# Low-rank transposes spread over later tiles, block numbers loaded by ScalarE, and another parity of the output rows' two buffers

## The chip, the core and the metric

The kernel runs on one core of one Trainium2 chip. The metric is the time of one execution on the device in microseconds (us). TensorE (PE) multiplies; its weight loads are recorded apart (PEld). VectorE (DVE), ScalarE (ACT) and GpSimd (POOL) do the elementwise work. SyncE (SP) computes nothing and issues most of the DMAs; ScalarE issues some.

## What is computed

Four residual layers over x of shape (32, 32, 512), 1024 rows of 512 in all:

```python
def reference(x, ...):
    x = x + _L0_cond_ref(x, itok_B_0_15, L0_cond_weights)      # per block of 32 rows: einsum('bct,bcd->bdt', x, weights[condition])
    x = x + _L1_cond_ref(x, itok_B_0_2, W, lora_A, lora_B_w)   # x @ W.T + 0.5 * (x @ lora_A[label]) @ lora_B_w.T
    x = x + _L2_cond_ref(x, L2_cond_weight, itok_B_3_7)        # x @ weight[adapter].T
    x = x + _L3_cond_ref(x, ...)                               # attention: q, k, v, norm, rope, 512 cached keys, 32 heads, Wo
    return x
```

In L0, L1 and L2 each of the 32 blocks picks its weights by a number that is given with the input. L3 is an attention with 32 query heads and 8 key heads over pages of a cache, and an output projection by Wo of 512 x 4096.

## The kernel before

The 1024 rows are eight tiles (TT) of 128 rows, four blocks (BT) of 32 to a tile; a row of 512 is four chunks (KC) of 128. Each engine has its own program, written out by hand, and engines wait for each other on semaphores. Products that need full precision are split into a high and a low part and done in three passes (`three_pass`, lines 107 to 111).

`stage_layers` does L0, L1, L2 and the tables of sines and cosines for L3. The list `uses` (lines 202 to 211) sets the order in which TensorE fills its eight PSUM banks, one bank to an entry, in turn; entry n waits until entry n-8 has been drained. TensorE, ScalarE and VectorE all walk through this list, so it sets the order of all three. Its entries are, for tile t: L0 (the product of L0), x1T (x turned), low (x times lora_A, line 372 on), lowT (the low-rank rows turned, line 382), L1 (the product of L1 with a last product of lowT with bw_t, line 392), x2T, L2 (line 402) and x3T.

On VectorE, `low` is two steps (lines 601 and 604), `lowT` a copy into low_t (line 608), and L0, L1, L2 an add to x (line 579). At the entry L1(0), ahead of its add, VectorE computes the angles (lines 507 to 518) and their reduction (lines 523 to 529), then reads block numbers and copies the first adapter weights (line 537). ScalarE at the same entry takes the sines (line 461) and copies its share of weights (line 434). GpSimd makes eight tables from the sines (line 341), after clearing and scaling bw_t (lines 330 and 333). These steps live in w1n, the room into which SP later fetches adapter weights: `fetch(0)` (line 291) waits for all eight tables, `fetch(1)` and `fetch(2)` for the last L1 product. L2(0) waits for the first fetch, L2(1) for the second.

At the start, SP issues the two rows of block numbers (lines 275 and 276), then x in four parts (line 280) and the weights of the later steps. ScalarE issues the table of L0's weights w0_all (line 418). VectorE and ScalarE wait for both rows of numbers and the table, then copy the blocks of L0's weights into place (lines 549 and 424), 16 copies each, four to a tile.

`stage_project_attend_output` projects, attends and multiplies by Wo. Between the attention and the end there are 32 units of output, four to a tile. For each unit SP loads the attention's rows and their scales (`load_o`, line 1021; `load_inv`, line 1027) into one of two buffers in room_a (`o_slot`), GpSimd multiplies them (line 1176), ScalarE takes the high part (line 1728), VectorE the low part (line 1537), and TensorE does 24 products (lines 109 to 111). The load of unit u+2 waits until the low part of unit u is done (o_lo_done). Unit 2 alone has a third buffer; unit 3 follows unit 1 in buffer 1. In the first units the high and low parts of Wo are made too (lines 1717 and 1521), from loads at line 653.

## Time and profile before

| | us |
|---|---|
| median of 3 runs | 1190.09 |
| lowest and highest | 1187.87, 1191.71 |
| the profiled execution | 1188.03 |
| its span | 1186.2 |
| TensorE busy | 1166.4 (98%) |
| VectorE busy | 851.5 (72%) |
| ScalarE busy | 687.1 (58%) |
| GpSimd busy | 727.6 (61%) |
| DMA, mean over the span | 239 GB/s |

The profile is of one execution. Its page gives the busy time of each engine; the timeline gives instructions in order of time, with the idle time ahead of an instruction and what released it in brackets. TensorE's granted clock is full throughout. A TensorE product is recorded with its whole length through the array, so consecutive ones overlap.

### The profile page before, as it was taken

The page shows a single profiled execution, that of the slowest core. Times are in us where ns is not written, and L with a number is a line of the kernel's source. Part 1 is how long each engine was busy: PE and PEld are TensorE (multiplying, and loading weights), DVE is VectorE, ACT ScalarE, POOL GpSimd, SP SyncE. Part 2 cuts the span into 40 slices and gives each one's busy share as a digit, 9 for nine tenths or more (in the row PEclk, how much of TensorE's full clock was granted, in tenths as well). Part 3 has the DMA queues.
Part 4 walks back from the last instruction along what each step waited for, and adds up shares of the span by engine and source line. Part 5 has one row for each costly group of instructions (what it writes and reads, how often), then busy time and mean ns, then how long its engine had stood idle before and what let it go on. Part 6 is the DMA issues. An engine that isn't in the chain of part 4 may idle for free.

```text
span 1186.2 us, 27883 instructions
## 1 busy us (share of the span) xinstructions
PE 1166.4 (98%) x8138; PEld 1030.1 (87%) x8138; DVE 851.5 (72%) x1746; ACT 687.1 (58%) x1647; POOL 727.6 (61%) x566
## 2 busy tenths in 40 slices
PE   7999999999999899999999999999999999999998
PEld 5746888888888799999999999999999998787877
DVE  7878687777866977877878778887788878722222
ACT  4175444344444577777777777777777778412111
POOL 1403999999999765555555555555555556344442
PEclk9999999999999999999999999999999999999999
...
GB/s 340 137 279 196 147 134 134 143 82 133 133 125 190 169 256 304 293 298 302 297 301 298 292 304 295 302 296 294 304 295 301 291 334 323 267 218 208 223 212 115
DMA packets 254401, 283.67 MB, mean 239 GB/s; under 512 B 56053, under 2 KB 208629, under 8 KB 254358
## 3 DMA queue, kind: packets, MB, share of 16 engines
...
HBM read 236.78 MB, written 46.27 MB: 239 GB/s over the span
## 4 chain that ended last, share of the span: by engine, by line
PE 52%; POOL 21%; issue 7%; DMA 5%; DVE 3%; ACT 2%; SPq 0%; ACTq 0%; POOLq 0%; DVEq 0%
PE early_pair L1237 19%; PE early_pair L1212 10%; PE early_pair L109 7%; PE early_pair L110 6%; PE early_pair L111 6%; POOL prj_rstd L1146 6%; POOL prj_qn L1148 5%; POOL prj_ta L1136 5%; DMA all_room_a<-inv_scratch 5%; PE early_pair L1244 3%; POOL prj_rs L1140 3%; POOL all_room_a L1176 2%; DVE out_o_lo L1537 2%; ACT out_o_hi L1728 1%; DVE out_wo_lo L1521 1%
## 5 line engine op out<-in xcount | busy, mean ns | idle before, releaser
L1604 ACT ACTIVATE att_prob<-att_neg,att_nmax 128x544 f32<-128x544 f32 x256 | 192.1, 750 | 115.9 <-DVE att_nmax L1369 91.0
L1369 DVE CUSTOM_DVE_ANT_1 att_neg<-att_mask,early_pair 128x576 f32<-128x576 f32 x256 | 192.1, 751 | 83.3 <-PE early_pair L111 67.5
L1156 POOL TENSOR_TENSOR att_k_lo<-all_room_a,att_k_hi 128x544 fp32r<-128x544 f32 x123 | 165.8, 1349 | 135.4 <-ACT att_k_hi L1630 135.4
L1156 POOL TENSOR_TENSOR att_k_lo<-att_kT,att_k_hi 128x544 fp32r<-128x544 f32 x128 | 173.9, 1359 | 105.5 <-ACT att_k_hi L1630 105.5
L1421 DVE COPY att_pT<-early_pair 128x512 f32<-128x512 f32 x256 | 175.8, 687 | 28.3 <-PE early_pair L1212 28.3
L109 PE MATMUL early_pair<-att_k_hi,att_q_lo 128*128 128x288 f32 (+1 forms) x512 | 168.8, 330 | 1.5 <-DVE att_nmax L1369 1.5
L1212 PE MATMUL early_pair<-all_ident,att_prob 128*128 128x128 f32 x1024 | 157.0, 276 | 0.0
L110 PE MATMUL early_pair<-att_k_lo,att_q_hi 128*128 128x288 f32 (+1 forms) x512 | 147.4, 288 | 0.0
L111 PE MATMUL early_pair<-att_k_hi,att_q_hi 128*128 128x288 f32 (+1 forms) x512 | 147.2, 288 | 0.0
L1176 POOL TENSOR_TENSOR all_room_a<-all_room_a 128x1024 f32<-128x1024 f32 x31 | 78.9, 2545 | 98.7 <-DMA all_room_a<-inv_scratch 98.7
L1237 PE MATMUL early_pair<-att_pT,att_vc 128*128 128x128 f32 x1024 | 135.4, 275 | 0.6 <-ACT att_ost L1761 0.6
L1237 PE MATMUL early_pair<-att_pT,all_room_b 128*128 128x128 f32 x1024 | 135.3, 275 | 0.0
L1212 PEld LDWEIGHTS early_pair<-all_ident,att_prob 128*128 128x128 f32 x1024 | 116.3, 140 | 20.9 <-issue 13.6
L1641 ACT ACTIVATE prj_sq<-early_pair 128x512 f32<-128x512 f32 x64 | 38.3, 599 | 165.5 <-PE early_pair L111 161.4
L1237 PEld LDWEIGHTS early_pair<-att_pT,att_vc 128*128 128x128 f32 x1024 | 124.5, 192 | 0.9 <-ACT att_ost L1761 0.8
L1237 PEld LDWEIGHTS early_pair<-att_pT,all_room_b 128*128 128x128 f32 x1024 | 124.5, 192 | 0.0
L1537 DVE TENSOR_TENSOR out_o_lo<-all_room_a,out_o_hi 128x1024 fp32r<-128x1024 f32 x31 | 41.1, 1325 | 107.7 <-ACT out_o_hi L1728 107.7
L1136 POOL TENSOR_TENSOR prj_ta<-prj_ta,prj_tb 128x640 f32<-128x640 f32 x64 | 101.1, 1579 | 9.1 <-DVE prj_tb L1471 9.0
L109 PE MATMUL early_pair<-out_wo_hi,out_o_lo 128*128 128x512 f32 x256 | 101.1, 395 | 2.5 <-DVE out_o_lo L1537 2.4
L1728 ACT ACTIVATE out_o_hi<-all_room_a 128x1024 fp32r<-128x1024 f32 x31 | 32.8, 1060 | 120.9 <-POOL all_room_a L1176 120.9
L111 PE MATMUL early_pair<-out_wo_hi,out_o_hi 128*128 128x512 f32 x256 | 99.8, 390 | 0.0
L110 PE MATMUL early_pair<-out_wo_lo,out_o_hi 128*128 128x512 f32 x256 | 99.8, 390 | 0.0
(164 smaller groups left out, 2928.7 us busy)
## 6 DMA issues: line engine op xcount, KB each, us to landing
all_room_a<-in_k_cache_t SPq DMA_DIRECT2D x256, 128.0 KB, 5.9
att_kT<-in_k_cache_t SPq DMA_DIRECT2D x256, 128.0 KB, 6.8
...
q_scratch<-prj_qst SPq DMA_DIRECT2D x64, 256.0 KB
att_vc<-in_L_cond_v_cache SPq DMA_DIRECT2D x128, 128.0 KB, 4.0
att_vc<-in_L_cond_v_cache ACTq DMA_DIRECT2D x128, 128.0 KB, 5.1
all_room_a<-o_scratch SPq DMA_DIRECT2D x31, 512.0 KB, 3.8
all_room_a<-inv_scratch SPq DMA_DIRECT2D x31, 512.0 KB, 5.5
```

The source lines that it names most:

```text
L109: pe.matmul(out, w_lo, x_hi, start=first, stop=False)
L110: pe.matmul(out, w_hi, x_lo, start=False, stop=False)
L111: return pe.matmul(out, w_hi, x_hi, start=False, stop=last)
L1136: g.tensor_tensor(ta[s][:], ta[s][:], tb[s][:], ALU.add).then_inc(pool_step, 1)
L1146: g.tensor_tensor(rstd[s][:], rs[s][:], power[:], ALU.pow).then_inc(pool_step, 1)
L1156: g.tensor_tensor(k_lo[j % SPLITS][:], kT[j // HK % 2][:, :, j % HK, :], f32(k_hi[j % SPLITS][:]), ALU.subtract).then_inc(k_split, 1)
L1176: g.tensor_tensor(o_n[s], o_n[s], inv_rows[s], ALU.mult).then_inc(o_scaled, 1)
L1212: t = pe.transpose(bank[:, c * P:(c + 1) * P], p[:, c * P:(c + 1) * P], ident[:])
L1237: pe.matmul(o, vc[s][:, c, cols], pT[j % 2][:, c, :], start=(c == 0 and j % PAIR == 0), stop=False)
L1369: v.tensor_tensor_reduce(halves[0], halves[1], scores_of(j, n)[:, :, 0:KA], 1.0, 3.0e38, ALU.add, ALU.min, nmax[j % 2][:]).then_inc(maxed, 1)
L1421: v.tensor_copy(pT[j % 2][:], pt[bank_of(j)][:].rearrange("p (c q) -> p c q", c=NCH)).then_inc(kept, 1)
L1604: act.activation(prob[j // GROUP % 2][:, j % GROUP, :], neg[j % 2][:, 0:KEYS], ACT.Exp, bias=nmax[j % 2][:, 0:1], scale=-1.0, accum_out=to ...
```

## The change

Four edits. First, the order of `uses`: lowT(t-3) follows low(t) from t = 3 on, and the last three follow L1(0). Since all three engines walk the list, VectorE's copies move with them, and the angles (and on ScalarE the sines) are now attached to L1(1). In L1 the waits for lowT and bw_t stand ahead of the last product only. Second, low_t no longer lies in the room that a_n, a_hi and a_lo had, which are still read by the later low products; it lies in a part of w2a. Third, ScalarE issues the two rows of block numbers, one ahead of w0_all and one behind it. Fourth, output unit 3 goes to buffer 0, unit 4 to buffer 1 and so on; its load waits for o_lo_done 1 instead of 2.

```diff
-        low_t = after_a.sb("low_t", [P, TT, P])
+        FETCHED = BT - 1
+        low_t = [w2a[:, i // KC, FETCHED, i % KC * P:(i % KC + 1) * P] for i in range(TT)]
@@ uses
-        uses += [("low", t) for t in range(TT)]
-        uses += [("lowT", t) for t in range(TT)]
-        uses += [("L1", t) for t in range(TT)] + [("x2T", 0)]
+        for t in range(TT):
+            uses += [("low", t)] + ([("lowT", t - 3)] if t >= 3 else [])
+        uses += [("L1", 0)] + [("lowT", t) for t in range(TT - 3, TT)]
+        uses += [("L1", t) for t in range(1, TT)] + [("x2T", 0)]
@@ SP
-                sp.dma_start(idx[:, 0, :], inp["itok_B_0_15"].rearrange("(a b) -> a b", a=1)).then_inc(idx_in, 16)
-                sp.dma_start(idx[:, 1, :], inp["itok_B_3_7"].rearrange("(a b) -> a b", a=1)).then_inc(idx_in, 16)
@@ TensorE, L1
-                        pe.wait_ge(lowt_ready, i + 1)
-                        pe.wait_ge(bw_ready, 1)
                         tok = slice(i * P, (i + 1) * P)
...
-                        end(u, pe.matmul(bank[:], low_t[:, i, :], bw_t[:], start=False, stop=True))
+                        pe.wait_ge(lowt_ready, i + 1)
+                        pe.wait_ge(bw_ready, 1)
+                        end(u, pe.matmul(bank[:], low_t[i], bw_t[:], start=False, stop=True))
@@ ScalarE
+                act.dma_start(idx[:, 0, :], inp["itok_B_0_15"].rearrange("(a b) -> a b", a=1)).then_inc(idx_in, 16)
                 act.dma_start(w0_all, inp["w0_t"]).then_inc(w0_all_in, 16)
+                act.dma_start(idx[:, 1, :], inp["itok_B_3_7"].rearrange("(a b) -> a b", a=1)).then_inc(idx_in, 16)
...
-                    elif kind == "L1" and j == 0:
+                    elif kind == "L1" and j == 1:
                         act.wait_ge(reduced, 2)
@@ VectorE
-                    if u == ("L1", 0):
+                    if u == ("L1", 1):
                         angles()
@@ output
         def o_slot(it, i):
-            return 2 if at_first(it) and i == 2 else i % 2
+            return i if at_first(it) and i <= 2 else (i + 1) % 2
+
+        def o_count(it, i):
+
+            return 1 if at_first(it) and i <= 2 else it * (O_UNROLL // 2) + (i + 1) // 2
@@ SP
                 sp.wait_ge(o_lo_done, 1)
-                sp.sem_inc(o_in[0], 16)
-                sp.sem_inc(inv_in[0], 16)
-                sp.wait_ge(o_lo_done, 2)
                 load_o(0, 3)
                 load_inv(0, 3)
+                sp.wait_ge(o_lo_done, 2)
                 load_o(0, 4)
                 load_inv(0, 4)
@@ GpSimd
-                    if s == 2:
-                        pool.wait_ge(o_in2, 16)
-                        pool.wait_ge(inv_in2, 16)
-                    else:
-                        pool.wait_ge(o_in[s], (it * (O_UNROLL // 2) + i // 2 + 1) * 16)
-                        pool.wait_ge(inv_in[s], (it * (O_UNROLL // 2) + i // 2 + 1) * 16)
+                    pool.wait_ge(o_in2 if s == 2 else o_in[s], o_count(it, i) * 16)
+                    pool.wait_ge(inv_in2 if s == 2 else inv_in[s], o_count(it, i) * 16)
```

VectorE's order at the end of the low-rank stage, before (lay_low_own and lay_low are the two steps of `low`, lay_low_t the copies of `lowT`, lay_row_i the first step of the angles):

```order
L601 SCALAR_TENSOR_TENSOR lay_low_own<-lay_lab_of,lay_lab,early_pair 128x160
L604 TENSOR_REDUCE lay_low<-lay_low_own 128x32
L608 COPY lay_low_t<-early_pair 128x128 x8
L507 TENSOR_SCALAR lay_row_i<-lay_pos_i 128x1
L508 CAST lay_base<-lay_row_i 128x1
L512 CAST lay_pos<-all_len_i 32x8 x4
```

The same place on VectorE after (all_room_a is x, so line 580 is the add of L1(0)):

```order
L602 SCALAR_TENSOR_TENSOR lay_low_own<-lay_lab_of,lay_lab,early_pair 128x160
L605 TENSOR_REDUCE lay_low<-lay_low_own 128x32
L609 COPY lay_w2a<-early_pair 128x128
L580 TENSOR_TENSOR all_room_a<-all_room_a,early_pair 128x512
L609 COPY lay_w2a<-early_pair 128x128 x3
L508 TENSOR_SCALAR lay_row_i<-lay_pos_i 128x1
L509 CAST lay_base<-lay_row_i 128x1
L513 CAST lay_pos<-all_len_i 32x8 x4
```

The add of L1(0) and three of the eight copies now stand between the last `low` and the angles; the other copies stand in the low-rank stage.

ScalarE's order at the start, after (before, lay_w2a, the table w0_all, stood alone ahead of the reading of the numbers from lay_idx):

```order
L417 DMA lay_idx<-in_itok_B_15 1x32
L418 DMA lay_w2a<-in_w_t 128x512
L419 DMA lay_idx<-in_itok_B_7 1x32
L262 TENSOR_LOAD lay_idx
L425 ISA
```

SP's queue at the start of the output stage, before (L653 loads Wo, L1021 rows, L1027 scales; units 3 and 4 stand behind one wait):

```order
L653 DMA out_wo5_2526<-in_wo_t 128x4x512 [waits pa_scored]
L1021 DMA all_room_a<-o_scratch 128x4x256 [waits pa_o_lo_done]
L1027 DMA all_room_a<-inv_scratch 128x4x256
L1021 DMA all_room_a<-o_scratch 128x4x256
L1027 DMA all_room_a<-inv_scratch 128x4x256
L653 DMA out_wo6_2527<-in_wo_t 128x4x512 [waits pa_exped]
```

The same place after (L654, L1026 and L1032 are the same loads):

```order
L654 DMA out_wo5_2526<-in_wo_t 128x4x512 [waits pa_scored]
L1026 DMA all_room_a<-o_scratch 128x4x256 [waits pa_o_lo_done]
L1032 DMA all_room_a<-inv_scratch 128x4x256
L1026 DMA all_room_a<-o_scratch 128x4x256 [waits pa_o_lo_done]
L1032 DMA all_room_a<-inv_scratch 128x4x256
L654 DMA out_wo6_2526<-in_wo_t 128x4x512 [waits pa_exped]
```

Each of the two units now has a wait of its own, unit 3 for o_lo_done 1 and unit 4 for o_lo_done 2.

## Rows read from the trace of the kernel before

**Rows 1.** Page, busy us (share of the span) and instructions of each engine.
```profile
PE 1166.4 (98%) x8138; PEld 1030.1 (87%) x8138; DVE 851.5 (72%) x1746; ACT 687.1 (58%) x1647; POOL 727.6 (61%) x566
```
**Rows 2.** Timeline, first 10 us: start, length, engine, line, operation [idle before, releaser].
```profile
0.72 0.35 SPq L275 DMA_DIRECT2D lay_idx<-in_itok_B  x1
1.43 1.95 SPq L280 DMA_DIRECT2D all_room_a<-in_x  x4
...
0.72 0.39 ACTq L418 DMA_DIRECT2D lay_w2a<-in_w_t  x1
...
4.99 3.01 DVE L549 COPY early_tabs<-lay_w2a 32x32 f32 x16 [4.99 <-issue]
...
6.27 3.75 PE L365 MATMUL early_pair<-all_room_a,early_tabs 128*128 128x512 f32 x4 [6.27 <-DMA all_room_a<-in_x]
```
**Rows 3.** DMA view, 0 to 8 us in 40 slices; issues, KB, us to landing.
```profile
GB/s 0 0 0 0 0 0 0 0 62 154 51 164 399 379 288 215 348 307 338 287 307 215 123 246 328 184 307 246 297 317 389 328 358 287 389 358 389 348 358 389
...
lay_w2a<-in_w_t ACTq DMA_DIRECT2D x1, 256.0 KB, 2.7
...
all_room_a<-in_x SPq DMA_DIRECT2D x1, 512.0 KB, 4.7
```
**Rows 4.** Timeline of TensorE, from the low-rank transposes to the end of L1(0).
```profile
30.62 0.94 PE L382 MATMUL early_pair<-all_ident,lay_low 128*128 128x128 f32 x7
...
33.19 0.47 PE L109 MATMUL early_pair<-lay_w,early_xT_lo 128*128 128x512 f32 x1 [1.08 <-DVE lay_low_t L608]
...
36.02 1.02 PE L392 MATMUL early_pair<-lay_bw_t,lay_low_t 128*128 128x512 f32 x2
```
**Rows 5.** Timeline of the other engines, from the copies to the first fetch.
```profile
31.58 1.66 DVE L608 COPY lay_low_t<-early_pair 128x128 f32<-128x128 f32 x8
...
34.44 0.75 DVE L512 CAST lay_pos<-all_len_i 32x8 f32<-32x8 int32 x4 [0.95 <-DMA lay_w1n<-in_L_cond_k_norm_w]
...
44.93 1.15 ACT L461 ACTIVATE lay_w1n<-lay_w1n 128x512 f32<-128x512 f32 x2 [15.51 <-DVE lay_w1n L529]
...
46.16 10.94 POOL L341 TENSOR_TENSOR early_tabs<-lay_w1n 128x512 f32<-128x512 f32 x8 [13.12 <-ACT lay_w1n L461]
...
57.28 0.40 SPq L291 DMA_DIRECT2D lay_w1n<-in_w_t  x1
```
**Rows 6.** DMA view: the first fetch, and the second and third.
```profile
lay_w1n<-in_w_t SPq DMA_DIRECT2D x1, 1024.0 KB, 5.5
...
lay_fetched<-in_w_t SPq DMA_DIRECT2D x2, 1024.0 KB, 6.7
```
**Rows 7.** Timeline: the last add of L1, and the first weight load of L2.
```profile
62.46 0.69 DVE L579 TENSOR_TENSOR all_room_a<-all_room_a,early_pair 128x512 f32<-128x512 f32 x1 [2.94 <-PE early_pair L392]
...
63.56 0.15 PEld L402 LDWEIGHTS early_pair<-lay_w2a,lay_low 128*32 128x32 f32 x4 [0.51 <-DVE all_room_a L579]
```
**Rows 8.** SP's queue ahead of output unit 3, and the landing of wo's fourth load.
```profile
995.94 0.75 SPq L653 DMA_DIRECT2D out_wo<-in_wo_t  x1
...
1004.78 0.37 SPq L1021 DMA_DIRECT2D all_room_a<-o_scratch  x1
...
out_wo<-in_wo_t SPq DMA_DIRECT2D x1, 1024.0 KB, 13.2
```
**Rows 9.** Timeline of GpSimd and VectorE around output unit 3.
```profile
1012.20 2.71 POOL L1176 TENSOR_TENSOR all_room_a<-all_room_a 128x1024 f32<-128x1024 f32 x1 [10.50 <-DMA all_room_a<-inv_scratch]
1016.38 3.00 POOL L1176 TENSOR_TENSOR all_room_a<-all_room_a 128x1024 f32<-128x1024 f32 x1 [1.47 <-DMA all_room_a<-inv_scratch]
...
1012.57 4.56 DVE L1521 TENSOR_TENSOR out_wo_lo<-out_wo,out_wo_hi 128x1024 fp32r<-128x1024 f32 x2
1017.05 3.41 DVE L1537 TENSOR_TENSOR out_o_lo<-all_room_a,out_o_hi 128x1024 fp32r<-128x1024 f32 x1
```
**Rows 10.** Timeline of TensorE: the starts of output units 3 and 5.
```profile
1020.52 0.50 PE L109 MATMUL early_pair<-out_wo_hi,out_o_lo 128*128 128x512 f32 x1 [0.82 <-DVE out_o_lo L1537]
...
1033.03 0.50 PE L109 MATMUL early_pair<-out_wo_hi,out_o_lo 128*128 128x512 f32 x1 [1.07 <-DVE out_o_lo L1537]
```

3 lines of the change are left out of this document (1 added, 2 removed).

## The prediction

> **What bounds the kernel now.** I read the page first: TensorE is busy for 98% of the span [rows 1], so only what moves TensorE's idle time or its start and end can show. The change adds and removes no work of weight (the eight transposes, copies and loads are the same), so the sum is about waits. I then read the order of the changed kernel, and went to the three places where it differs: the first 10 us (timeline and DMA view), 30 to 64 us (timeline by engine), and 1000 to 1035 us, where the output stage starts. What lies between (projection and attention, some 900 us) is untouched, and everything there waits for its predecessor and for nothing at a fixed time, so a shift at its front is carried to the end.
>
> In the front stage TensorE waits three times for something that the change touches. It starts at 6.27, released by the landing of x [rows 2]. It pauses between the transposes of the low-rank rows, which start at 30.62, and the first L1 product at 33.19 [rows 4]. And the first L2 product loads its weights at 63.56 [rows 7]. In the output stage it waits 0.82 us before unit 3 and 1.07 us before unit 5 [rows 10].
>
> **The change, part by part.**
>
> (1) The block numbers. Before, SP issues both index loads from 0.72 on and x from 1.43; ScalarE issues the table of weights w0_all at 0.72 [rows 2]. After, x is issued at 0.72, so 0.71 earlier; w0_all follows one index load (0.35 us of issue), and the second index load follows w0_all. VectorE's placing of the blocks waits for all three. w0_all landed 2.7 us after its issue, that is at 3.4, while x had the engines only for the last part of this, and the traffic from 2 us on is some 300 GB/s [rows 3]. Now 256 KB of w0_all and the first 512 KB of x are in flight together from about 1.7 on: 768 KB at 300 GB/s end at 4.3, and the index load ends behind the w0_all part of them. The table and both numbers are there somewhere between 0.4 us later than before (the issue alone) and 1.5 us later (all of x's first part ahead of them). I take 1.0. So VectorE's copies start at 6.0 instead of 4.99; four of the 16 (3.01 us [rows 2]) make a tile, so TensorE's first product starts at 6.8, not 6.27: **+0.55 us**, called d below, from -0.15 to +1.05. That x lands at 5.4 instead of 6.1 (4.7 us after issue [rows 3]) is of no use, since it is no longer what comes last. A pure gain of 0.7 is a rival below. The tile loop behind it runs on VectorE's adds and splits, one after another, so d goes through.
>
> The Trainium skill, DMA: Bandwidth & Descriptors, section on queues, rings and completion order, says that each ring's descriptors are taken in order and that an engine drains a packet of one queue row before it turns to another; it speaks against this part: the index load would stand behind w0_all in ScalarE's ring and both behind x's share. By it d would be at its upper end, 1.05, and the sum 0.5 us more; the rows show only that the two queues share one rate.
>
> (2) The transposes. Before, eight in one run from 30.62 and eight VectorE copies from 31.58, 1.66 us in all, then L1(0) at 33.19 [rows 4, 5]. After, five stand in the low-rank stage or right behind it, 0.12 us each (0.94 for seven), so L1(0) starts at 30.62 + 0.6 = 31.2: 2.0 earlier. Its last product starts 2.83 later [rows 4], at 34.0. bw_ready, which GpSimd makes behind the last low product, is asked for only there, 2.8 us into L1(0), and I take it as hidden. Three transposes follow L1(0), 0.35 us. L1's eight tiles then end 2.0 - 0.35 = 1.65 us earlier than before. Taken alone that is the gain of the change: **-1.65 us**.
>
> (3) What this delays. In VectorE's order the add of L1(0) and three copies now stand ahead of the angles, which stood right behind the eight copies. The add waits for the end of L1(0): 34.0 + 1.02 [rows 4] = 35.05. The add is 0.69 [rows 7], three copies 3 x 0.21 [rows 5], so VectorE is free at 36.4, and the casts of the positions start at 36.65. Before they started at 34.44, and 0.95 of that was waiting for a load [rows 5], which is no longer late. The chain behind them has no slack until its end: angles and reductions on VectorE, the sines on ScalarE at 44.93, the eight tables on GpSimd from 46.16 to 57.10, each step released by the one before, and then SP's first fetch of adapter weights at 57.28, which waits for the tables since it overwrites their inputs [rows 5]. All of it moves by 36.65 - 34.44 = 2.2: fetch issued at 59.5. It lands 5.5 us after issue [rows 6]: 65.0. L2(0) waits for it at its head. Before, it landed at 62.8, 0.8 us ahead of the need at 63.56 [rows 7]; after, TensorE would be ready at 63.56 - 1.65 = 61.9 and waits 3.1 us, until 65.05. Net of (2) and (3): 65.05 - 63.56 = **+1.5 us**. So the gain of (2) is not only lost; the start of L2 moves back. The times here are all before d, which is added once.
>
> The second and third fetch wait for the last L1 product. They now go out 1.65 earlier and the first one 2.2 later, so they come close behind it. Two fetches issued together took 6.7 us in the mean [rows 6]. If they hold the first one back, it lands up to 1.2 later; I take the undisturbed 5.5, since the first one still has the head start.
>
> (4) The output rows. Unit 3 goes to buffer 0, so its load waits for the split of unit 0 instead of unit 1 and is issued at about 1002.8 instead of 1004.78 [rows 8]; unit 4's goes out 0.9 earlier. But the fourth load of wo, issued at 995.94, took 13.2 us and landed at 1009.1 [rows 8], so the engines were full until then, and unit 3's rows came through 3 us later for 1 MB: GpSimd began its scaling at 1012.20 and that of unit 4 at 1016.38 [rows 9]. An earlier place in a full queue brings little: I take 0.4 of the 2.0. Then VectorE: two splits of wo from 1012.57 take 4.56 and the split of unit 3 takes 3.41 from 1017.05 on [rows 9], each longer where GpSimd works beside it; moving GpSimd earlier moves this overlap and does not remove it. So unit 3 is ready some 0.4 earlier and TensorE's 0.82 shrinks by that: **-0.4 us**. The bounds are 0 (the queue alone decides) and -1.9 (both waits [rows 10] gone, 0.82 + 1.07). From unit 5 on both parities have the same distances as before.
>
> The sum: 0.55 + 1.5 - 0.4 = **+1.65 us**. The profiled execution took 1188.03 with a span of 1186.2; it becomes 1189.7 with a span of 1187.8. The median of the runs is 1190.09, 2.1 above the profiled execution, and the forecast is against the median: 1190.09 + 1.65 = **1191.7**.
>
> **The rivals.**
> A. The fetch is no bound: the angle chain has slack that I don't see, and L1's gain is kept. For it: the row at 63.56 names no fetch as what released L2(0) [rows 7]. Against: the landing was only 0.8 us ahead of the need. Time: 1190.09 + 0.55 - 1.65 - 0.4 = 1188.6.
> B. The early load of unit 3 removes both waits of the output stage: 1190.09 + 0.55 + 1.5 - 1.9 = 1190.2. For it: 2.0 us of earlier issue is as much as both waits. Against: the full engines until 1009.1.
> C. The first fetch shares its way with the second and third. From 0.1 us of added landing on it is felt in full, since L2(0) waits for nothing else; at 6.7 us instead of 5.5 it is +1.2, and with the index load at its worst (+0.5) and no gain at the output (+0.4) the kernel is slower: 1193.8.
> D. The start of x decides the first product, as it did before, and the index load costs nothing: d = -0.7, 1190.09 - 0.7 + 1.5 - 0.4 = 1190.5.
> E. The change doesn't do what it says in the low-rank stage: VectorE falls behind with its interleaved copies and TensorE waits for it. Five copies of 0.21 [rows 5] are 1.05 us, and all of it on the path would give 1192.7; it is inside the range and gets no chance of its own beside the forecast's.
>
> **How the numbers follow.** Forecast 0.50, A 0.12, B 0.14, C 0.14, D 0.10. All of them lie within 4 us of each other. A measurement of this kernel can tell 0.3% from no change, 3.6 us: below 1186.5 is faster, above 1193.7 slower. Only A with B's gain reaches the first (1187.1) and only C the second; with the spread of the three runs (3.8 us from lowest to highest) I give faster 0.07, same 0.80, slower 0.13. The range goes from A with B's gain, 1187.1, to C with 0.5 of that spread, 1194.3.
>
> **What would show it.** In the new profile: VectorE's first block copy at about 6.0 and TensorE's first product at 6.8; L1(0) at 31.2 + 0.55 = 31.8; the casts of the positions at 37.2; GpSimd's tables until about 59.9; the first fetch issued near 60.1; TensorE idle for about 3 us ahead of the first L2 product, released by the fetch's DMA, and this product at 65.6; unit 3 of the output with a wait of about 0.4 instead of 0.82 and unit 5 still waiting. The prediction is wrong if L2(0) starts before 63.5, if the copies start before 5.4, or if unit 5 has no wait.

## The result, and the profile after

| | before | after |
|---|---|---|
| median of 15 runs | 1190.09 us | 1195.78 us |
| lowest, highest | 1186.72, 1197.75 | 1190.24, 1201.75 |
| ratio of the two, 95% interval | | 1.0043 (1.0025 to 1.0061) |
| profiled execution, its span | 1188.03, 1186.2 | 1193.41, 1191.6 |

The kernel became slower by 5.7 us (3.0 to 7.3 by the interval), where +1.65 was forecast; the range ended at 1194.3. The ratios, here and below, leave out executions more than 1.5% above the fastest of their kernel; the medians hold all. The fifteen executions of either kernel lie 0.9 to 1.0% apart from lowest to highest. In the eighteen profiled executions of this document, the stretch from the first product of the attention to the first of the output took 598.7 to 603.3 us, and the output 182.3 to 196.8, in kernels that differ little or not at all there. At the first product of the projection, the four kernels that were profiled twice repeated to 0.4, 0.9, 1.1 and 3.0 us. So the experiments below are read mostly by times of single instructions up to there, and a difference of 1 us between two single executions says little unless the instructions behind it are named.

The start, which [rows 2] showed before. Timeline of the kernel after, ScalarE's queue, SP's queue, VectorE and TensorE:

```profile
0.73 0.55 ACTq L417 DMA_DIRECT2D lay_idx<-in_itok_B  x1
1.31 0.38 ACTq L418 DMA_DIRECT2D lay_w2a<-in_w_t  x1
1.72 0.36 ACTq L419 DMA_DIRECT2D lay_idx<-in_itok_B  x1
...
0.72 1.99 SPq L279 DMA_DIRECT2D all_room_a<-in_x  x4
...
7.40 3.02 DVE L550 COPY early_tabs<-lay_w2a 32x32 f32 x16 [7.40 <-issue]
...
8.27 1.19 PE L364 MATMUL early_pair<-all_room_a,early_tabs 128*128 128x512 f32 x1 [8.27 <-DVE early_tabs L550]
```

VectorE's block copies start 2.4 us later than before, TensorE 2.0 later, and what releases TensorE is now the copies and not x. The DMA view, 0 to 8 us (40 slices of 0.2 us; then issues, KB, us from issue to landing), against [rows 3]:

```profile
GB/s 0 0 0 0 0 0 0 0 1 102 133 266 358 389 430 389 420 379 420 379 338 410 410 410 379 358 318 389 318 338 297 430 369 430 389 389 420 399 420 381
...
lay_w2a<-in_w_t ACTq DMA_DIRECT2D x1, 256.0 KB, 4.9
```

The table w0_all, in the place lay_w2a, took 4.9 us instead of 2.7, from a later issue: it lands at 6.2 instead of 3.4.

From the low-rank rows to the first fetch, which [rows 4, 5] showed. Timeline of the kernel after, by engine:

```profile
33.17 0.48 PE L109 MATMUL early_pair<-lay_w,early_xT_lo 128*128 128x512 f32 x1
...
37.06 0.69 DVE L580 TENSOR_TENSOR all_room_a<-all_room_a,early_pair 128x512 f32<-128x512 f32 x1 [2.66 <-PE early_pair L391]
37.66 0.68 DVE L609 COPY lay_w2a<-early_pair 128x128 f32<-128x128 f32 x3
...
50.34 10.92 POOL L340 TENSOR_TENSOR early_tabs<-lay_w1n 128x512 f32<-128x512 f32 x8 [14.78 <-ACT lay_w1n L462]
...
61.44 0.40 SPq L290 DMA_DIRECT2D lay_w1n<-in_w_t  x1
```

L1(0) starts at 33.17, as before, in spite of the late start: the spread transposes gave 2.0 back. Then VectorE waits 2.66 us for the end of L1(0) with the angles queued behind, and the tables and the fetch come 4.2 later than in [rows 5].

The head of L2, which [rows 7] showed. Timeline of TensorE, then the stretches of 60 to 72 us (length, TensorE busy, granted clock, DMA share, GB/s), kernel after:

```profile
66.97 0.89 PE L401 MATMUL early_pair<-lay_w2a,lay_low 128*32 128x512 f32 x3 [3.48 <-issue]
...
64.00:66.00 2.00, 0.00 (x0) 1.00 1.17 367
...
67.00:68.00 1.00, 1.00 (x8) 0.61 0.98 342
68.00:69.00 1.00, 1.00 (x8) 0.50 0.96 367
69.00:70.00 1.00, 1.00 (x8) 0.50 1.05 399
70.00:71.00 1.00, 1.00 (x12) 0.69 1.04 408
71.00:72.00 1.00, 1.00 (x15) 1.00 0.87 338
```

The stretch from 64 to 66 us has no product at all. TensorE had nothing to do for 3.48 us, and then worked some 3 us at the lower of its two clock levels (0.50, that is 1.2 GHz). The add of L2(0) started 5.4 us behind its first product, 3.7 before.

The output, which [rows 10] showed. Timeline of TensorE, kernel after, the first product of unit 3:

```profile
1026.67 0.50 PE L109 MATMUL early_pair<-out_wo_hi,out_o_lo 128*128 128x512 f32 x1 [0.79 <-DVE out_o_lo L1536]
```

Unit 5 starts at 1038.05 without a wait in this execution, where it had waited 1.07.

The account of the profiled pair, as lateness of the kernel after at one place after the other:

| place | before | after | late by |
|---|---|---|---|
| first L0 product | 6.27 | 8.27 | 2.0 |
| L1(0) | 33.19 | 33.17 | 0.0 |
| casts of the angles | 34.44 | 38.62 | 4.2 |
| fetch 0 issued | 57.28 | 61.44 | 4.2 |
| first L2 product | 63.59 | 66.97 | 3.4 |
| first product of the projection | 100.13 | 104.88 | 4.75 |
| first product of the attention | 404.41 | 409.17 | 4.76 |
| first product of the output | 1003.10 | 1009.27 | 6.2 |
| end of the span | 1186.2 | 1191.6 | 5.4 |

### The profile page after: what moved, and what is told of

Same layout as the page of the kernel before. It is cut to its first block, busy times and chain, and to the rows that moved or that the text cites. A ratio compares the mean times of both kernels' runs of the same rounds, so it can differ in the third digit from the quotient of the medians.

```text
span 1191.6 us, 27884 instructions
## 1 busy us (share of the span) xinstructions
PE 1168.2 (98%) x8138; PEld 1030.4 (86%) x8138; DVE 855.9 (72%) x1746; ACT 686.6 (58%) x1647; POOL 725.5 (61%) x566
## 3 DMA queue, kind: packets, MB, share of 16 engines
q10 hardware_dynamic: 17092, 48.76, 13.4%
## 4 chain that ended last, share of the span: by engine, by line
PE 55%; POOL 19%; issue 7%; DMA 3%; DVE 3%; ACT 1%; SPq 1%; ACTq 0%; POOLq 0%; DVEq 0%
PE early_pair L1236 19%; PE early_pair L1211 10%; PE early_pair L109 8%; PE early_pair L110 8%; PE early_pair L111 8%; POOL prj_rstd L1149 6%; POOL prj_qn L1151 5%; POOL prj_ta L1139 4%; PE early_pair L1243 3%; DMA all_room_a<-inv_scratch 3%; POOL prj_rs L1143 3%; POOL all_room_a L1175 1%; DVE out_wo_lo L1520 1%; DVE out_o_lo L1536 1%; ACT out_o_hi L1727 1%
## 5 line engine op out<-in xcount | busy, mean ns | idle before, releaser
L1211 PEld LDWEIGHTS early_pair<-all_ident,att_prob 128*128 128x128 f32 x1024 | 116.4, 140 | 20.9 <-issue 13.9
```

Of the source, the lines that this page charges most:

```text
L1211: t = pe.transpose(bank[:, c * P:(c + 1) * P], p[:, c * P:(c + 1) * P], ident[:])
```

## The experiments

Theory at this point: four terms. The block numbers cost 2.0 at the start. The add and copies ahead of the angles cost 1.4 net of what the earlier L1 gives. TensorE's idle time ahead of L2 costs about 1.4 more by the granted clock. The output order gives 0.8. Rivals: one of the parts is without price, or the clock fell for another reason.

**All results in one place.** Medians and ratios to the kernel before (same chip, same hour), then single times of the profiled execution: first L0 product; from there to low(0); idle time of TensorE ahead of L2(0); whether the granted clock fell there; start of the projection.

| kernel | median, ratio (95%) | L0 | to low(0) | idle | clock | projection |
|---|---|---|---|---|---|---|
| before | 1190.09 | 6.27 | 13.6 | 0.3 | 1.00 | 100.1 |
| after | 1195.78, 1.0043 (1.0025 to 1.0061) | 8.27 | 13.8 | 3.5 | 0.50 | 104.9 |
| after_again | 1196.68, 1.0058 (1.0034 to 1.0081) | 8.47 | 14.6 | 3.3 | 1.00 | 104.0 |
| numbers_on_sp | 1193.27, 0.9989 (0.9937 to 1.0042) | 5.83 | 13.7 | 3.6 | 0.50 | 102.5 |
| numbers_on_sp_2 | 1193.62, 1.0015 (0.9986 to 1.0043) | 5.89 | 13.6 | 3.3 | 0.50 | 102.2 |
| lowrank_only | 1192.33, 0.9984 (0.9933 to 1.0035) | 5.82 | 13.7 | 3.7 | 0.50 | 102.5 |
| numbers_only | 1194.54, 0.9995 (0.9943 to 1.0046) | 8.42 | 16.5 | 0.5 | 1.00 | 105.3 |
| numbers_only_2 | one execution | 8.47 | 13.6 | 0.3 | 1.00 | 102.3 |
| output_only | 1188.77, 0.9946 (0.9895 to 0.9996) | 5.79 | 14.1 | 0.3 | 1.00 | 100.2 |
| both_first | one execution | 7.85 | 14.1 | 0.3 | 1.00 | 102.5 |
| w0_first | one execution | 8.75 | 13.4 | 0.3 | 1.00 | 102.5 |
| x_behind | one execution | 7.34 | 13.9 | 0.3 | 1.00 | 101.5 |
| busy_wait | 1196.88, 1.0060 (1.0036 to 1.0084) | 8.47 | 14.6 | filled | 1.00 | 104.3 |
| sp_busy_wait | 1196.05, 1.0016 (0.9981 to 1.0051) | 5.99 | 13.6 | filled | 1.00 | 100.8 |
| split_later | 1195.11, 1.0027 (1.0003 to 1.0051) | 8.40 | 14.5 | 3.6 | 0.50 | 105.8 |
| angles_early | 1192.98, 1.0022 (1.0001 to 1.0044) | 8.43 | 14.5 | 2.3 | 0.50 | 104.6 |
| angles_early_sp | 1187.99, 0.9982 (0.9952 to 1.0011) | 5.98 | 13.5 | 1.4 | 1.00 | 98.5 |
| angles_early_sp_2 | 1188.64, 0.9984 (0.9961 to 1.0008) | 6.25 | 13.6 | 2.1 | 1.00 | 99.7 |

In the first four (numbers_on_sp, numbers_only, lowrank_only, output_only) the kernel before itself ran from 1188 to 1213, so those ratios settle little.

### One part undone, or one alone

**numbers_on_sp**: the kernel after, with the two loads back on SP.

```diff
+sp.dma_start(idx[:, 0, :], ...).then_inc(idx_in, 16)
+sp.dma_start(idx[:, 1, :], ...).then_inc(idx_in, 16)
 x_rows = ...
-act.dma_start(idx[:, 0, :], ...).then_inc(idx_in, 16)
 act.dma_start(w0_all, ...)
-act.dma_start(idx[:, 1, :], ...).then_inc(idx_in, 16)
```

> The kernel after with one part undone: the two loads of block numbers issued by SP ahead of x again. Theory (four terms: start +2.0, tables and fetch 0 late +1.4, granted clock at L2(0) about +1.4, output order -0.8): VectorE's block copies back at 5.0 us, first L0 product at 6.3, L1(0) at 31.2, fetch 0 at 59.4, L2(0) at 65.0 with the granted clock still about 0.5 in its stretch; time 2.0 us below the kernel after, about +2.0 to +3.5 on the kernel before (ratio 1.0017 to 1.003). Rival A (the numbers' issuer is without price, the start moved for another reason): copies stay at 7.4 us and the ratio stays at 1.0043. Rival B (the low-rank order costs nothing once the start is right): ratio 0.9993 or less.

Measured: copies at 4.95, first product at 5.83, L1(0) at 30.7, fetch 0 at 58.99, L2(0) at 64.6 with the clock at 0.50 behind it, projection at 102.5 (104.9 in the kernel after). Theory, in every place to 0.5 us; rival A falls by the copies. The ratio, 0.9989 with a wide interval, would fit rival B; it falls by the projection, 2.4 us later than in the kernel before with the start in order. Undoing this part takes 2.4 us away at the projection.

**numbers_only**: the kernel before, with the numbers' loads alone as in the kernel after (the reverse of the diff above), and **numbers_only_2**, a second profiled execution of the same kernel.

> The kernel before with one part alone: the two loads of block numbers issued by ScalarE around w0_all. Theory: the transfer of w0_all starts only when x's share is drained, copies at 7.4 us, first L0 product at 8.3, everything behind it 2.0 later (L1(0) at 35.2, fetch 0 at 59.3, L2(0) at 65.6), no stretch of low granted clock at L2(0), since TensorE waits there no longer than before; ratio 1.0017 (1.0010 to 1.0022). Rival A: a delay at the start is absorbed at the wait for fetch 0 and the ratio is 1.000. Rival B: the start costs the granted clock too, and the ratio is over 1.0025.

> The same kernel as numbers_only, looked at once more: there the first product came 2.15 late, but low(0) 5.1 late, with VectorE's sixteen block copies taking 4.80 us instead of 3.0 (one of them 1.43) and TensorE's load of weights waiting on nothing the profile shows. If that belongs to the start's new order it comes again (low(0) at 24.5 to 25.5); if it was that execution's own, the copies take 3.0 us and low(0) starts at 22.0, as in the kernel after.

Measured: the first product at 8.42 and 8.47, as expected. But the projection came 5.2 us late the first time and 2.1 the second. The difference arises ahead of low(0), which came 16.5 and 13.6 us behind the first product. Clock 1.00 and no long wait at L2(0) in both, so rival B falls; and the delay of the start goes through undiminished to the projection, so rival A falls. The 2.9 us more were not expected by anything, and are taken up under split_later.

**lowrank_only**: the kernel before, with the spread transposes and their rows' new place alone.

```diff
-        uses += [("low", t) for t in range(TT)]
-        uses += [("lowT", t) for t in range(TT)]
-        uses += [("L1", t) for t in range(TT)] + [("x2T", 0)]
+        for t in range(TT):
+            uses += [("low", t)] + ([("lowT", t - 3)] if t >= 3 else [])
+        uses += [("L1", 0)] + [("lowT", t) for t in range(TT - 3, TT)]
+        uses += [("L1", t) for t in range(1, TT)] + [("x2T", 0)]
```

> The kernel before with one part alone: the low-rank rows' transposes spread over later tiles. Theory: L1(0) starts 2.0 earlier (31.2), the casts of the angles start at 36.6, fetch 0 at 59.4, TensorE idle over 3 us ahead of L2(0) at 65.0, granted clock about 0.5 there; in all +1.4 for the fetch and +1.4 for the clock, ratio 1.0024 (1.0012 to 1.003). Rival A (the gain of the earlier L1 outweighs): ratio 0.999. Rival B (the granted clock fell because of the late start, not of the wait): clock 1.00 in L2(0), ratio 1.0012.

Measured: L1(0) at 30.66, casts 36.12, fetch 0 at 58.95, L2(0) at 64.7, granted clock 0.81, 0.50, 0.50, 0.50 from 64 to 68, projection 102.5: 2.4 late. Rival B falls: the start was as before and the clock fell. Rival A falls by the projection's time, though the ratio alone (0.9984 with a wide interval) would have let it stand.

**output_only**: the kernel before, with the output rows' parity alone (o_slot, o_count and SP's order of loads).

> The kernel before with one part alone: the output rows' buffers alternate in the other parity from the fourth unit. Theory: nothing moves up to the output stage; there the wait of the sixth unit goes (1.46 to about 0.36) and smaller ones come later, in all -0.8, ratio 0.9993 (0.9988 to 0.9998). Rival A: the waits only move, ratio 1.0000. Rival B: the output order is what costs the kernel after its time, ratio over 1.001.

Measured: nothing moved ahead of the output. There the profiled execution waited as before [rows 10] at units 3 and 5, and more behind them. Timeline of TensorE, output_only, the first products of the two units:

```profile
1021.36 0.50 PE L109 MATMUL early_pair<-out_wo_hi,out_o_lo 128*128 128x512 f32 x1 [0.79 <-DVE out_o_lo L1535]
...
1033.86 0.51 PE L109 MATMUL early_pair<-out_wo_hi,out_o_lo 128*128 128x512 f32 x1 [1.09 <-DVE out_o_lo L1535]
```

Added up over the output stage, TensorE's waits for o_lo are 2.4, 2.4, 2.7, 2.8, 3.1, 3.4 and 12.1 us in the seven profiled executions with the old order, and 1.2, 1.8, 2.3, 2.4, 2.8, 2.8, 2.9, 3.6, 4.8, 6.6 and 6.7 us in the eleven with the new one. The medians are 2.8 and 2.8. The kernel's ratio here (0.9946, interval to 0.9996) was taken against a kernel before that ran high at that hour, 1197 in the median, so it is no gain that can be relied on. What the new order gave in the profile of the kernel after was that execution's own: neither the theory's -0.8 nor rival B is shown, rival A (the waits only move) fits best.

Where they move to can be read unit by unit. In none of the seven executions with the old order did TensorE wait at unit 2, and in five it waited 0.8 at unit 3. With the new one it waited 0.2 to 1.3 us at unit 2 in seven of eleven, and there not at unit 3. GpSimd's scaling of unit 3, brought forward, then begins before VectorE's low part of unit 2, which takes 1.9 to 3.3 us beside it and 1.23 without. Timeline of after_again, GpSimd, VectorE and TensorE:

```profile
1016.66 2.41 POOL L1175 TENSOR_TENSOR all_room_a<-all_room_a 128x1024 f32<-128x1024 f32 x1 [6.81 <-DMA all_room_a<-inv_scratch]
...
1017.61 2.54 DVE L1536 TENSOR_TENSOR out_o_lo<-all_q,out_o_hi 128x1024 fp32r<-128x1024 f32 x1 [2.13 <-ACT out_o_hi L1727]
...
1020.21 0.50 PE L109 MATMUL early_pair<-out_wo_hi,out_o_lo 128*128 128x512 f32 x1 [1.04 <-DVE out_o_lo L1536]
```

### What makes the start late

Three more orders of the start, on the kernel before, one execution each. **both_first**: ScalarE issues both numbers, then w0_all. **w0_first**: w0_all, then both numbers. **x_behind**: as in the kernel after, and SP holds x back:

```diff
+sp.wait_ge(idx_in, 32)
 x_rows = inp["x"].rearrange("(t b) c h -> (b c) t h", b=BT)
```

> The kernel before with both loads of numbers issued by ScalarE ahead of w0_all (second number load ahead of, not behind, the 256 KB). Theory (w0_all waits for x's share because x is issued first): w0_all lands about as late as in the kernel after (6.2) or 0.4 later, copies at 7.4 to 7.9. Rival (the second number load behind w0_all is what is late, w0_all itself is not): copies at 5.6 to 6.0.

> The kernel before with ScalarE issuing w0_all first (about 0.7, together with x by SP) and the two number loads behind it. Theory (who is issued first is served first): w0_all's packets run beside x's or ahead of them, w0_all lands at 3.5 to 4.5, the numbers behind it are late, at 4.5 to 5.5: copies at 5.5 to 6.5. Rival (x on SP's row goes first whatever ScalarE issues): copies at 7.4 or later.

> The kernel before with ScalarE issuing numbers, w0_all, numbers, and SP holding x back until both number loads have landed. Theory: with x out of the way the numbers land at about 3.0 and w0_all at about 3.5 to 4.0, VectorE's copies start at 5.0 or a little earlier; x part 0, issued at 3.0, lands at about 5.5 to 6.0, so the first L0 product stays at 6.3 to 6.8 and later x parts set the L0 products behind it, about 1 to 2 us late at the low-rank stage. Rival (ScalarE's issues are slow in themselves): copies stay at 7.4.

Measured, with SP's x issued at 0.72 but for x_behind (3.90):

| kernel | w0_all issued, us to landing | copies start | first product |
|---|---|---|---|
| before | 0.72, 2.7 | 4.99 | 6.27 |
| after | 1.31, 4.9 | 7.40 | 8.27 |
| both_first | 1.57, 5.2 | 6.97 | 7.85 |
| w0_first | 0.73, 4.2 | 7.87 | 8.75 |
| x_behind | 1.30, 2.8 | 5.50 | 7.34 |

The queues' packets in the first 3.8 us of the kernel after (q1 is SP's, q10 ScalarE's; packets, MB, share):

```profile
q1 hardware_dynamic: 336, 0.66, 50.9%
q10 hardware_dynamic: 3, 0.00, 0.2%
```

By then 0.66 MB had passed on SP's queue, and of w0_all, issued 0.59 us behind the first part of x, next to nothing. From then on the two queues shared. Queues of the kernel after, 3.8 to 5.0 us:

```profile
q1 hardware_dynamic: 120, 0.25, 53.0%
q10 hardware_dynamic: 107, 0.22, 50.1%
```

In both_first w0_all is issued at 1.57 instead of 1.31. There SP's queue moved 0.92 MB up to 4.6 us against 4 packets of ScalarE's, and from 5.0 to 5.4 w0_all went nearly alone:

```profile
q10 hardware_dynamic: 64, 0.13, 93.2%
q1 hardware_dynamic: 12, 0.01, 9.1%
```

With x out of the way w0_all takes 2.8 us again, as it did when x was issued 0.71 behind it; with x ahead of it, 4.9 and 5.2. In both_first what releases VectorE is w0_all:

```profile
6.97 3.02 DVE L549 COPY early_tabs<-lay_w2a 32x32 f32 x16 [6.97 <-DMA lay_w2a<-in_w_t]
```

In the kernel after w0_all lands at 6.2 and the copies start at 7.40: the profile names nothing that released them, and what is left is the second row of numbers, which stands behind w0_all, and the reading of it. The kernel before says the same: w0_all had landed at 3.4 there, and the copies started at 4.99. From the issue of the second row to the first copy it is 3.85 us before (issued at 1.14), 3.8 in x_behind (1.71), and 5.7 in the kernel after (1.72). Of the 2.4 us by which the copies are late, 0.6 is therefore the later issue and 1.8 the longer way. L0 reads the first row only (`idx[0:1, 0, b]` in `states`), but the engines wait for both (`idx_in`, 32); a wait for the first row alone was not tried, and by both_first, where the copies waited for w0_all until 6.97, it would give about 0.4 (an estimate).

In w0_first, w0_all lands earliest of the three orders with x at 0.72 (at 4.9) and the copies start latest: both rows of numbers are issued behind it, and behind the first parts of x. From 3.0 to 4.2 us the two queues, whose first loads were issued together, took 50% and 43% there.

So in these five orders the loads passed about in the order in which they were issued, over both queues, and those issued together shared. Large loads that the copies do not need yet delay the 128 bytes that they wait for. What holds w0_all's first packets back for 2.4 us in the kernel after is not shown by the traces.

The theory of both_first holds by w0_all, which landed at 6.8; the copies came at 6.97, earlier than expected, since nothing was behind it. That of x_behind holds with the copies at 5.50 and not at 5.0, and the first product at 7.34 and not 6.8 at most, since x was issued 0.9 later than I took it for. For w0_first both parts failed: w0_all landed at 4.9 and not by 4.5, and the copies were expected by 6.5 and started at 7.87, which I had for the rival's time, but through the numbers and not through w0_all alone. No order with the numbers on ScalarE reaches SP's 5.0 and 5.9; x_behind comes nearest with the copies and then waits for x.

By the Trainium skill (DMA: Bandwidth & Descriptors, Queues, rings and completion order) each ring is worked off in order, SP and ScalarE have one row of rings each on the same engines, and an engine changes between rows only at a packet's end. The order within ScalarE's ring agrees with w0_first, and the equal shares from 3.8 to 5.0 us agree with the taking of turns. But turns alone would let w0_all share from its first microseconds on, and 0.66 MB went ahead of it.

### GpSimd and VectorE at 10 us

The 2.9 us that numbers_only had lost behind its first product, and 0.9 in after_again, go with this. Start and length of GpSimd's split of a, timeline of after_again, then VectorE's copies, and the copies' single lengths (ns: shortest, median, longest; first and last start):

```profile
10.04 0.71 POOL L324 CAST lay_a_hi<-lay_a_n 128x640 fp32r<-128x640 f32 x1 [6.47 <-DMA lay_a_n<-in_lora_a_t]
10.84 1.53 POOL L326 TENSOR_TENSOR lay_a_lo<-lay_a_n,lay_a_hi 128x640 fp32r<-128x640 f32 x1
...
7.59 4.81 DVE L550 COPY early_tabs<-lay_w2a 32x32 f32 x16 [7.59 <-issue]
...
L550 DVE COPY early_tabs<-lay_w2a x16: 169/172/1423, 7.6 to 11.0; 32x32 f32 x16
```

One copy of 0.17 us took 1.42, and its end is that of GpSimd's subtraction. Over all executions with a late start: where GpSimd began at 9.84, 9.87, 9.97 or 10.04, the sixteen copies took 4.69 to 4.83 us; where it began at 10.26, 10.32 or 10.53, 3.02. In w0_first, where the copies ran from 7.87 on and GpSimd began at 10.37, they took 3.45. With the start as before GpSimd begins at 11.2 or later and the copies are done by 8.1. So the late start brings VectorE's copies to where GpSimd is at work, and with x issued earlier GpSimd's input a_n lands earlier too (cast at 10.26 in the kernel after, 11.52 before). In the four executions with slow copies TensorE then waited 0.84 to 1.27 us for VectorE's add behind them, and in the others not. Timeline of after_again:

```profile
13.18 0.66 PE L368 MATMUL early_pair<-all_ident,all_room_a 128*128 128x128 f32 x4 [1.27 <-DVE all_room_a L580]
```

**split_later**: the kernel after, with GpSimd waiting for VectorE's four tiles.

```diff
+pool.wait_ge(w0_placed["dve"], len(W0_TILES["dve"]))
 pool.wait_ge(a_in, 16)
 g.tensor_copy(a_hi[:], a_n[:]).then_inc(a_split, 1)
```

> The kernel after with one wait more: GpSimd begins its split of the low-rank matrix a only when VectorE has placed its four tiles of blocks. Theory (the two engines hold each other up while both work from 10 to 12.4 us): the sixteen copies take 3.0 us (4.8 in after_again), GpSimd's cast starts at 10.6 and its subtraction ends at 13, long before low(0); low(0) comes 13.6 to 13.8 behind the first L0 product instead of 14.6, and the kernel is 0.9 us faster than after_again was, ratio about 1.004. Rival (the copies are slow for another reason, such as DMA traffic): 4.8 us all the same, low(0) 14.6 behind.

Measured: GpSimd's cast at 10.61, the sixteen copies in 3.02 us:

```profile
10.61 0.71 POOL L325 CAST lay_a_hi<-lay_a_n 128x640 fp32r<-128x640 f32 x1 [7.04 <-DVE early_tabs L551]
...
7.52 3.02 DVE L551 COPY early_tabs<-lay_w2a 32x32 f32 x16 [7.52 <-issue]
```

The collision is the cause of the slow copies, and TensorE's wait behind them is gone too. But low(0) still came 14.5 us behind the first product, not 13.7, and the projection started at 105.8, so that half of the expectation failed. What was slower is TensorE itself. Lengths of the products at the start (all products before 14 and before 20 us; shortest, median, longest in ns), split_later and then the kernel after:

```profile
L365 PE MATMUL early_pair<-all_room_a,early_tabs x6: 842/1062/1193, 8.4 to 13.7; 128*128 128x512 f32 x6
```
```profile
L364 PE MATMUL early_pair<-all_room_a,early_tabs x16: 592/595/1192, 8.3 to 19.8; 128*128 128x512 f32 x16
```

A product of this size takes 1.06 us at first in every kernel and 0.59 later, though the granted clock reads 1.00 throughout; the change came before the product at 12.64 in the kernel after, only after 13.7 in split_later, and in numbers_only, where the slow copies had left TensorE idle for 0.95 us at 12.2, not before 17. The idle time alone does not do it: in after_again and busy_wait, with 1.3 and 1.2 us of it, the change had come before 12. With the start as before it came at about 10. So the time from the first product to low(0) is 13.4 to 14.1 us without a collision or a delay of that change, 14.5 or 14.6 with one of them, and 16.5 in the one execution that had both. What decides the moment was not tried. What the collision costs the kernel is therefore read from the traces and not shown by this run: 14.6 in after_again against 13.8 in the kernel after, 0.8 us, one execution each.

The Trainium skill (SBUF — State Buffer, Who interferes with whom) has it that VectorE's copies can run in modes that use two pairs of ports, one of them shared with GpSimd, and that this pair is taken by one of the two for a whole instruction while the other stands still. No row names the mode of these copies. The lengths agree: the long copy is the length of the subtraction, not a slower copy.

### The granted clock at L2(0)

**busy_wait**: the kernel after, with TensorE at work in the wait; **after_again**, the kernel after, beside it. **sp_busy_wait** and **numbers_on_sp_2** are the same pair with the numbers on SP.

```diff
 pe.wait_ge(x2_turned, i + 1)
+for _ in range(28 if i == 0 else 0):
+    pe.transpose(bank[:, 0:P], ident[:], ident[:])
 pe.wait_ge(w2_fetched[i % RING], (i // RING + 1) * 16)
```

> The kernel after itself, beside the three below on the same chip. Theory: up to the projection it is the same to 0.5 us (copies 7.4, L1(0) 33.2, fetch 0 at 61.4, L2(0) at 67.0, granted clock 0.5 in 68 to 70, projection at 104.9); the +1.4 us that the first profile showed between the first attention tile and the output is that execution's own and comes back in another size or sign. Rival: it comes back at +1.4 (a lasting cost of the change in the attention part).

> The kernel after with TensorE kept busy while it waits for fetch 0: 28 transposes of the identity into the bank of L2(0), whose first product overwrites it; nothing else moves. Theory (the idle time ahead of L2 is what halves the granted clock): L2(0) starts at 67.0 as before or up to 0.3 later, its granted clock is 1.00, its products keep 0.43 us apart, the add of L2(0) comes 3.7 behind its start instead of 5.4, and the projection starts 1.2 to 1.6 earlier than in the kernel after (103.4). Rival A (the clock fell for another reason, such as DMA traffic or heat): 0.50 in 68 to 70 all the same. Rival B (L2's tiles wait for VectorE's and ScalarE's picks anyway): clock 1.00 but the projection no earlier.

> The same kernel as numbers_on_sp (start as before, TensorE idle 3.4 us ahead of L2(0)), beside the next one. Theory: nearly all executions have a mean granted clock below 1.000 (six of six the first time), since the clock falls to half at L2(0); projection at 102.5; ratio 1.002. Where an execution of it keeps the clock, the projection is at 101.1. Rival: the share of executions below 1.000 is that of the kernel before (13 of 35).

> The same with TensorE kept busy by 28 transposes of the identity until fetch 0 has landed. Theory (the idle time is what halves the clock): granted clock 1.00 from 64 to 72, first L2 product at 64.6 to 64.9, its tiles at full pitch, projection at 101.0 (102.5 without), at most a third of the executions below 1.000; ratio 0.0014 under that of numbers_on_sp_2. Rival: clock 0.50 at L2(0) all the same.

Measured. Stretches of TensorE (as above), after_again, numbers_on_sp_2 and sp_busy_wait:

```profile
66.00:67.00 1.00, 0.00 (x0) 1.00 1.03 397
...
68.00:69.00 1.00, 1.00 (x12) 1.00 1.00 328
```
```profile
64.00:65.00 1.00, 0.74 (x8) 0.79 1.00 322
65.00:66.00 1.00, 1.00 (x11) 0.50 0.96 315
66.00:67.00 1.00, 1.00 (x8) 0.50 1.01 391
67.00:68.00 1.00, 1.00 (x8) 0.51 1.03 399
```
```profile
64.00:65.00 1.00, 1.00 (x11) 1.00 1.01 383
65.00:66.00 1.00, 1.00 (x16) 1.00 1.02 385
66.00:67.00 1.00, 1.00 (x16) 1.00 0.93 344
```

In after_again the clock stayed at 1.00 behind 3.29 us of idle time, against the theory. Then L2's eight tiles took 35.0 us from the first product to the start of the last add. So they did in all five executions with the new order of transposes where the clock stayed (34.99 to 35.00), and in the six where it fell it was 36.6 or 36.7. So a fall costs 1.7 at this place, and the idle time alone does not always bring it. Against the kernel before, where the same stretch took 35.3, that is 1.4. Over all profiled executions it fell in six of seven with 2.3 to 3.7 us of idle time there, and in none of the eleven with 2.1 us or less, or with the time filled. In the clean pair, sp_busy_wait reached the projection at 100.8, numbers_on_sp_2 at 102.2: 1.4 less, as expected (1.7 by the clock, and L2(0) 0.3 later behind the transposes of the identity). busy_wait against after_again shows nothing (104.3 and 104.0), since after_again had not lost the clock; L2(0) came at 68.1 and 67.8 in them and not at 67.0, both behind the slow copies.

The same is seen elsewhere in these executions, where nothing was changed for it. Behind the projection TensorE waited for 2.6 us or more six times: at 412 us in numbers_on_sp and both_first (3.1), at 1080 and 1176 in numbers_only_2 (3.4 and 3.1), at 1169 in numbers_on_sp_2 (3.0) and at 1167 in sp_busy_wait (2.6). The clock fell to 0.50 behind all but the one in numbers_on_sp_2, and behind none of the waits of 1.2 to 1.8 us. TensorE in sp_busy_wait, first its timeline and then stretches:

```profile
1166.51 0.50 PE L110 MATMUL early_pair<-out_wo_hi,out_o_lo 128*128 128x512 f32 x1 [2.59 <-DVE out_o_lo L1539]
```
```profile
1168.00:1169.00 1.00, 1.00 (x4) 0.50 0.93 294
```

The mean granted clock of each execution says the same with more of them. Below 1.000 (the fall at L2(0) alone, some 3 us at 0.50, is 0.001) were:

```
long idle time:   after 15 of 15, after_again 9 of 12, numbers_on_sp 6 of 6 and 12 of 12,
                  lowrank_only 6 of 6, split_later 12 of 12
2.3 us:           angles_early 4 of 12
filled:           busy_wait 3 of 10, sp_busy_wait 8 of 12
short:            numbers_only 1 of 6, output_only 1 of 6, angles_early_sp 3 and 2 of 12,
                  before 37 of 81
```

Together 60 of 63 with a long idle time. The kernels in the other rows lose the clock elsewhere too, as just seen. That may be why sp_busy_wait has eight of twelve, where a third at most was expected, and why its median is no lower than numbers_on_sp_2's; without more profiles it is not shown. The shift of 1.4 us is shown by the single times, not by the medians.

The Trainium skill (TensorE: Matmul & The Clock Gate, HAM oscillation) describes this: products that wait for a transfer come back at half clock. It spoke against this change, and I had not weighed it. The traces agree in six executions of seven.

### The angles

**angles_early**: the kernel after, with VectorE's angles and reductions ahead of the add of L1(0); the picks stay behind the copies. **angles_early_sp**: the same with the numbers on SP, run twice.

```diff
-                    if u == ("L1", 1):
+                    if u == ("L1", 0):
                         angles()
                         reduce(0, 0.0, 0.0)
                         reduce(1, 0.25, 0.5 * np.pi)
+                    if u == ("L1", 1):
                         adapter = adapters(mybir.EngineType.DVE)
```

> The kernel after with VectorE's angles and reductions moved ahead of the add of L1(0) and of the last three copies of low-rank rows; the first picks stay behind them. Theory: the casts start when their loads have landed (about 36.4, from 38.6), fetch 0 goes out at 59.2, L2(0) starts at 64.7 instead of 67.0, TensorE's idle time ahead of it falls from 3.5 to about 1.2; the granted clock then stays at 1.00, and the projection starts 3.5 to 3.7 earlier than in the kernel after (101.3). Rival A: the clock falls after 1.2 us too, projection at 102.5. Rival B: L1(5), whose bank and last product wait for the add and the copies now behind the angles, stops TensorE, and nothing is gained.

> The same with the block numbers issued by SP again: the version that the runs point to. Theory: copies 5.0, L1(0) 30.7, casts at 34.2, fetch 0 at 57.0, L2(0) at 62.5 (63.6 in the kernel before), projection at 99.1 (100.1 before), and 0.8 less in the output stage: 1.9 us below the kernel before, ratio 0.9984. Rival A (fetches 1 and 2, issued 1.9 earlier, hold fetch 0 back): L2(0) at 63.6 or later, ratio 0.9993. Rival B (clock falls in the short wait): ratio 0.9996.

> The version that the runs point to (numbers by SP, spread transposes, angles ahead of the add of L1(0), output order of the kernel after) once more. Theory: projection at 98.5 again (100.1 in the kernel before), L2(0) at 62.3 with clock 1.00, at least 0.5 less in the output stage; ratio 0.9980 (0.9970 to 0.9995). Rival (the first gain was the mood of the executions): ratio 1.000.

Measured. In angles_early the casts still started at 38.6 and fetch 0 at 61.4, only 1.0 earlier against the start of L1(0) than in the kernel after (27.4 instead of 28.3): there the loads of the angles' inputs set the casts, 2.2 later than I had put them. ScalarE issued the last of them at 30.64 (27.65 in the kernel before), and it took 7.9 us to land (6.7 before):

```profile
38.63 0.76 DVE L513 CAST lay_pos<-all_len_i 32x8 f32<-32x8 int32 x4 [3.11 <-DMA lay_w1n<-in_L_cond_k_norm_w]
```

So what stood in [rows 5] as 0.95 us of waiting for a load is the next bound once the add is out of the way. TensorE idled 2.27 us, and the clock fell all the same:

```profile
66.66 0.63 PE L401 MATMUL early_pair<-lay_w2a,lay_low 128*32 128x512 f32 x3 [2.27 <-issue]
...
68.00:69.00 1.00, 1.00 (x10) 0.50 0.98 361
```

So neither the theory nor rival A was tested as put, since both took an idle time of 1.2 us; what is shown is that 2.27 us was enough. With the numbers on SP the fetch goes out at 56.74 and 57.95, TensorE idles 1.40 and 2.10 us, and the clock stays:

```profile
62.31 0.63 PE L403 MATMUL early_pair<-lay_w2a,lay_low 128*32 128x512 f32 x3 [1.40 <-ACT lay_low L473]
```

The projection starts at 98.5 and 99.7 (100.1 before), where 99.1 and 98.5 were expected; the second time the casts waited for their load until 35.12 instead of 33.93. The gain of 0.8, then 0.5, expected in the output did not come (182.9 and 184.3 us from its first product to the end, 183.1 before). The medians of twelve runs, 1187.99 and 1188.64, are 2.6 and 2.2 below those of the kernel before in the same hours, the ratios 0.9982 and 0.9984, and both intervals reach past 1. This version is 7 to 9 us below the kernel after, and better than the kernel before by about as much as can just not be shown.

## Why the prediction was wrong

The sum had four terms: +0.55 for the start, -1.65 and what this delays, together +1.5, and -0.4 for the output, in all +1.65. Measured: +5.7 between the medians, and +5.4 between the profiled spans.

**(1) The start: mis-sized, 0.55 against 2.0.** This is the first of the two steps that failed. I let w0_all and x share one rate and took the middle, 1.0 for the copies, where they moved by 2.4; even the upper bound, "all of x's first part ahead of them", was too low. By 5.4 us, when w0_all's packets were through, SP's queue had moved 1.0 MB and not 512 KB. And the bound counted the bytes, and not that the second row of numbers and its reading come behind them again (7.40 - 6.2 = 1.2 us). The rule of the Trainium skill that I had quoted against myself was the better guide, and w0_all had landed 2.7 us after issue before only because x was not ahead of it (2.8 in x_behind, 4.9 with x ahead). Rival D (x decides, -0.7) is out.

**What the late start met: not seen.** VectorE's copies moved to where GpSimd splits a, and in four of six profiled executions with the start's order of the kernel after (split_later apart) they took 1.7 to 1.8 us more. I looked for who waits for the copies, and not for who works beside them at the new time. TensorE waited 0.8 to 1.3 us for it in those four. It did not in the profiled execution of the kernel after, so none of the 5.4 us there is from this.

**(2) and (3) The transposes and the fetch: right.** L1(0) at 31.2 was expected without the start's delay; lowrank_only has it at 30.7 from a first product 0.45 earlier than before. Casts 36.65 (36.12 there), fetch 59.5 (58.95), L2(0) 65.05 (64.7). Between the kernels before and after L2(0) is 3.4 late, of which 2.0 is the start: 1.4 where 1.5 was forecast. Rival A (the chain has slack) is out. Rival C is out too: L2(0) started 5.5 us behind the issue of the first fetch, which was taken to land in 5.5, with the other two 1.3 us behind it. The idle time of 3 us ahead of L2(0) was forecast and came, 3.48. One reading there was wrong without a price: the load that the casts waited for [rows 5] was taken to be no longer late, and in angles_early it moved with ScalarE's issue and set the casts again.

**What the idle time did: missing, the second step that failed.** The prediction named the wait of 3.1 us, and let TensorE come back from it at full speed: the term stood at nothing, without a reason. The granted clock fell to 0.50, and L2's tiles took 36.7 us instead of 35.0 in the same order and 35.3 before. In a forecast that rests on a new wait of TensorE this needs a term.

**(4) The output: -0.4 forecast, about 0 shown.** Unit 5's wait, which should have stayed, was gone in the profile of the kernel after, by which the prediction had called itself wrong; it is there in output_only and in seven more of the eleven executions with the new order. Unit 3's was 0.79 in the kernel after, not 0.4. The sum of the waits has the same median with either order. Rival B is out. The reasons given were that an earlier place in a full queue brings little, and that moving GpSimd moves its overlap with VectorE and does not remove it; the waits at unit 2 show the second at work.

The sum with the measured terms: 2.0 + 1.4 + 1.4 = 4.8 at the start of the projection, where the profiled pair is 4.75 apart, and 0 for the output, against 5.4 and 5.7 measured at the end. In the profiled pair the rest is +1.4 in the attention and -0.8 in the output. For the 5.7 of the medians the rest is not accounted for; collisions at the start are a part of it in some executions. The 1.4 us that the first profile lost between attention and output came back in after_again as 1.0 us in 599.7 against 598.7, and the same stretch ran from 598.9 to 603.3 in kernels that differ in nothing there: it belongs to the executions. The kernel before was the fastest of the eighteen there, which is luck of its profile.

**The chances.** Slower by over 0.3% got 0.13; it was argued from the range of the terms, and the two missing effects both had one sign, and so had the error of the output term (0.4 us). Both effects came from making an engine wait or move, and I gave such effects no width.
